# Attention scores from fp16 splits of scaled latents and queries, with two small jobs moved between VectorE and ScalarE

## The reference

```python
q_c = layernorm(x) @ Wq_c.T + bq_c                        # 192 latents
q = (q_c @ Wq_up.T + bq_up).reshape(b, s, 32, 192)
kv = layernorm(x) @ Wkv_c.T + bkv_c                       # 64 key/value latents, 64 rope columns
k_nope, v = split(kv[..., :64] @ Wkv_up.T + bkv_up)       # 128 and 128 per head
k = concatenate([k_nope, kv[..., 64:]])                   # rope columns shared by the heads
scores = einsum('bhqd,bhkd->bhqk', q, k) / sqrt(192)
o = einsum('bhqk,bhkv->bhqv', softmax(scores), v)
x = x + einsum('bhsv,Hv->bsH', o, Wo) + bo
x = x + ffn(layernorm(x))
```

## Time and profile before

| what | value |
|---|---|
| median of 3 runs | 1978.44 us (1977.9 to 1979.36) |
| the profiled execution | 1978.39 us, its span 1976.4 us |
| PE busy | 1937.1 us, 98% |
| DVE busy | 1622.0 us, 82% |
| ACT busy | 1353.8 us, 68% |
| POOL busy | 1102.3 us, 56% |
| mean granted TensorE clock | 0.992 of 2.4 GHz |

### The profile page before, as it was taken

How to read it: one execution, slowest core, us unless ns; L and a number is a source line. 1 busy time by engine, 2 the same in 40 slices (tenths; PEclk the granted TensorE clock), 3 DMA queues, 4 the chain that set the end, 5 groups by cost and what they waited for, 6 DMA issues and landing times. The chain is left out here.

```text
span 1976.4 us, 37173 instructions
## 1 busy us (share of the span) xinstructions
PE 1937.1 (98%) x11014; PEld 1441.7 (73%) x11014; DVE 1622.0 (82%) x2585; ACT 1353.8 (68%) x2488; POOL 1102.3 (56%) x1215
## 2 busy tenths in 40 slices
PE   7999999999999999999999999999999999999798
PEld 6767777777777777777777777777777777777576
DVE  6588888888888888888888888888888888888665
ACT  4367777777777777777777777777777777777443
POOL 3336566565665665655656656656656566565710
PEclk9899999999999999999999999999999999999899
DMA  5521111111111111111111111111111111111211
GB/s 201 194 62 32 43 40 34 43 34 41 44 33 43 40 35 43 36 39 43 34 42 43 32 43 40 35 43 36 40 43 32 43 39 35 43 34 33 75 43 43
DMA packets 74308, 95.19 MB, mean 48 GB/s; under 512 B 25856, under 2 KB 48416, under 8 KB 74272
## 3 DMA queue, kind: packets, MB, share of 16 engines
q1 hardware_dynamic: 70176, 86.33, 17.1%
q0 software_dynamic: 4096, 8.40, 1.2%
HBM read 83.95 MB, written 10.75 MB: 48 GB/s over the span
## 5 line engine op out<-in xcount | busy, mean ns | idle before, releaser
L832 DVE TENSOR_TENSOR PTL<-X,PTH 128x512 f16<-128x512 f32 x1024 | 658.6, 685 | 147.8 <-ACT PTH L783 142.0
L783 ACT ACTIVATE PTH<-X 128x512 f16<-128x512 f32 x1024 | 554.3, 594 | 281.5 <-PE X L692 281.5
L848 DVE TENSOR_REDUCE mx<-S 128x1 f32<-128x1024 f32 x512 | 623.6, 1218 | 3.0 <-PE S L712 3.0
L798 ACT ACTIVATE prob<-S,shift 128x1024 f32<-128x1024 f32 x512 | 574.2, 1121 | 1.7 <-DVE shift L856 1.6
L692 PEld LDWEIGHTS X<-ident,prob 128*128 128x128 f32 x4096 | 469.2, 141 | 120.6 <-issue 53.3
L692 PE MATMUL X<-ident,prob 128*128 128x128 f32 x4096 | 538.1, 274 | 5.3 <-ACT prob L798 5.3
L710 PE MATMUL S<-kvTH,qeH 128*128 128x512 f32 x1024 | 445.5, 435 | 1.6 <-DVE qeL L837 1.6
L712 PE MATMUL S<-kvTH,qeL 128*128 128x512 f32 x1024 | 406.0, 396 | 0.0
L711 PE MATMUL S<-kvTL,qeH 128*128 128x512 f32 x1024 | 401.9, 392 | 0.0
L658 POOL TENSOR_TENSOR onormH<-osum,recip_row 128x512 fp32r<-128x512 f32 x128 | 198.5, 1551 | 288.7 <-ACT osum L806 288.7
L643 POOL TENSOR_TENSOR wvH<-wv,unit_tile 128x128 fp32r<-128x128 f32 x128 | 57.4, 448 | 393.4 <-PE V L763 387.7
(11 more groups left out here) (202 smaller groups left out, 1972.2 us busy)
## 6 DMA issues: line engine op xcount, KB each, us to landing
recip_row<-row_scratch SPq DMA_DIRECT2D x128, 256.0 KB, 4.2
weff<-weff_scratch SPq DMA_DIRECT2D x128, 192.0 KB, 4.0
wv<-in_wv POOLq DMA_DIRECT2D x128, 64.0 KB, 3.7
raw<-in_raw SPq DMA_DIRECT2D x8, 772.0 KB, 5.2
weff_scratch<-w_split SPq DMA_DIRECT2D x8, 768.0 KB, 4.8
x<-in_x SPq DMA_DIRECT2D x4, 1024.0 KB, 6.8
x_all<-in_x SPq DMA_DIRECT2D x3, 1024.0 KB, 6.8
out<-y SPq DMA_DIRECT2D x3, 1024.0 KB, 4.2
```

Source lines behind the costliest of these rows:

```text
L783: nc.scalar.activation(PTH[p][:, part:part + 4, unit * P:(unit + 1) * P], X[:, k % 2, :].rearrange("p (k c) -> p k c", k=4), ACT.Copy).the ...
L798: nc.scalar.activation(prob[u][:], S[:, u % 2, :], ACT.Exp, bias=shift[:, col:col + 1], accum_out=rs[:, col:col + 1]).then_inc(probs_ready, 1)
L832: v.tensor_tensor(PTL[p][at], X[:, k % 2, :].rearrange("p (k c) -> p k c", k=4), PTH[p][at], ALU.subtract).then_inc(low_out, 1)
L848: v.reduce_max(mx[:, col:col + 1], S[:, u % 2, :], AX.X).then_inc(max_ready, 1)
```

## The change

The scores' operands become fp16: `kvTH`, `kvTL`, `qeH` and `qeL`, which were fp32r (fp32 storage). So that fp16 can hold them, the key latents and the queries are scaled by powers of two, and the exponential undoes it by a factor `unscale`.

- `prepare`: all 128 key latents are scaled on ACT where they are read out (`read_projected`), with `scale` and `kbias` made on DVE before. To scale the queries, DVE takes the largest entry of each group's effective weights (two `reduce_max` in `split_absorbed`), and a chain of small steps between DVE and PE (`reach_of_queries`, `scale_of_queries`, three matmuls of one or 128 columns) makes `qscale` and `unscale`.
- `attention`, queries: ACT writes the scaled queries twice from `O`, once as fp32 `qef` and once as fp16 `qeH`, both with a factor and a bias from memory. DVE forms `qeL` from these two, in phase 3 instead of phase 1, and no longer reads `O`. PE waits for `q_high` instead of `q_low` before it writes over `O`.
- `attention`, shift: DVE writes the row's `top` (the same kind of instruction as before). ACT makes `shift` from it by an activation on 128x1, waits for its own result, and runs the exponential with `unscale` as a factor from memory.

```diff
@@ -145,7 +154,9 @@
...
@@ -256,24 +268,29 @@
...
-                pe.wait_ge(wabs_ready, 2)
+                pe.wait_ge(wabs_ready, 1)
                 for k in range(KT):
-                    last = mm(psN[:, UN * KVL:UN * KVL + 1], wabs[:, k, :], ones[:], start=(k == 0), stop=(k == KT - 1))
+                    last = mm(psN[:, B0:B0 + 1], wabs[:, k, 0:P], ones[:], start=(k == 0), stop=(k == KT - 1))
                 last.then_inc(bound_done, 1)
                 pe.wait_ge(wlL_ready, 1)
...
-                pe.wait_ge(diag_ready, 1)
                 for u in range(UN):
-                    last = mm(psN[:, u * KVL:(u + 1) * KVL], kvf[0:KVL, u * P:(u + 1) * P], diag[:], start=True, stop=True)
+                    last = nc.tensor.transpose(psN[:, u * KVL:(u + 1) * KVL], kvf[0:KVL, u * P:(u + 1) * P], ident[0:KVL, 0:KVL])
                 last.then_inc(n_done, 1)
 
             def turn(n, nxt):
                 if nxt is None:
                     project(n, (0,))
+                    pe.wait_ge(wabs_ready, 3)
+                    for c in (1, 2):
+                        for k in range(KT):
+                            last = mm(psT[0][:, c - 1:c], wabs[:, k, c * P:(c + 1) * P], ones[:], start=(k == 0),
+                                      stop=(k == KT - 1))
+                    last.then_inc(qbound_done, 1)
                     absorb(n, 0)
                     project(n, (1,))
...
@@ -304,6 +321,16 @@
...
+                if n == 1:
+                    pe.wait_ge(q_step, REACH)
+                    pe.wait_ge(n_out, NB + 1)
+                    mm(psN[:, B0 + 1:B0 + 2], ones_all[:], reach[:, 0:1], start=True, stop=True).then_inc(reach_done, 1)
+                if n == 2:
+                    pe.wait_ge(q_step, TERM)
+                    pe.wait_ge(proj_out, 3 * NB)
+                    mm(psB[0:1, 0:P], term[:], ident[:], start=True, stop=True).then_inc(term_turned, 1)
+            pe.wait_ge(q_step, TOP)
+            mm(psN[:, B0 + 2:B0 + 3], ones_all[0:1, :], top[0:1, :], start=True, stop=True).then_inc(top_spread, 1)
...
                 nc.scalar.activation(wlH[:], wl[:], ACT.Copy).then_inc(wlH_ready, 1)
-                for half in range(2):
-                    nc.scalar.activation(wabs[:, :, half * KVL:(half + 1) * KVL], wl[:, :, 0:KVL],
-                                         ACT.Abs).then_inc(wabs_ready, 1)
-                nc.scalar.activation(pbabs[:], pb[:, 3:4], ACT.Abs).then_inc(wabs_ready, 1)
+                nc.scalar.activation(wabs[:, :, 0:P], wl[:, :, 0:P], ACT.Abs).then_inc(wabs_ready, 1)
+                nc.scalar.activation(pbabs[:], pb[:], ACT.Abs).then_inc(wabs_ready, 1)
                 read_turned(n, range(UN))
+                nc.scalar.activation(wabs[:, :, P:3 * P], wl[:, :, P:3 * P], ACT.Abs).then_inc(wabs_ready, 1)
...
                 for j in which:
                     out, src, hi = ((kvf, psA, "kvTH"), (qaf, psB, "qaH"), (qbf, psC, "qbH"))[j]
                     act.wait_ge(proj_done, 3 * n + j + 1)
-
-                    nc.scalar.activation(out[:], src[:], ACT.Identity, bias=pb[:, j:j + 1])
-                    nc.scalar.activation(keep[hi][:, tok], src[:], ACT.Identity, bias=pb[:, j:j + 1]).then_inc(proj_out, 1)
+                    if j == 0:
+                        act.wait_ge(k_scaled, 1)
+                    factor, bias = (scale[:, 0:1], kbias[:, 0:1]) if j == 0 else (1.0, pb[:, j:j + 1])
+                    nc.scalar.activation(out[:], src[:], ACT.Identity, bias=bias, scale=factor)
+                    nc.scalar.activation(keep[hi][:, tok], src[:], ACT.Identity, bias=bias, scale=factor).then_inc(proj_out, 1)
...
                 high, low = split[i][:, :, 0, :], split[i][:, :, 1, :]
+                v.reduce_max(wmax[:, ds(g, 1), 0], full[:, :, 0, :], AX.XY, apply_absolute_value=True)
+                v.reduce_max(wmax[0:QB, ds(g, 1), 1], full[0:QB, :, 1, :], AX.XY, apply_absolute_value=True)
                 v.tensor_copy(high, full[:, :, 0, :]).then_inc(half_done, 1)
                 v.tensor_copy(split[i][0:QB, :, 2, :], full[0:QB, :, 1, :]).then_inc(half_done, 1)
...
-            def scales_of_values():
+            def scales_of_latents():
...
-                v.tensor_scalar(diag[:], ident[0:KVL, 0:KVL], scale[0:KVL, 0:1], None, ALU.mult).then_inc(diag_ready, 1)
+                v.tensor_scalar(kbias[:], pb[:, 0:1], scale[:, 0:1], None, ALU.mult).then_inc(k_scaled, 1)
+
+            def reach_of_queries():
+
+                dve.wait_ge(qbound_done, 1)
+                v.scalar_tensor_tensor(out=bound[:, 1:3], in0=psT[0][:, 0:2], scalar=NORM_MAX, in1=pbabs[:, 1:3],
+                                       op0=ALU.mult, op1=ALU.add).then_inc(q_step, 1)
+                dve.wait_ge(split_done, groups + 1)
+                v.reduce_max(wtop[:], wmax[:].rearrange("p g s -> p s g"), AX.X).then_inc(q_step, 1)
+                dve.wait_ge(q_step, 2)
+                v.tensor_tensor(reach[:, 1:2], wtop[:, 1:2], bound[:, 2:3], ALU.mult).then_inc(scale_out, 1)
+                dve.wait_ge(scale_out, 3)
+                v.scalar_tensor_tensor(out=reach[:, 0:1], in0=wtop[:, 0:1], scalar=bound[:, 1:2], in1=reach[:, 1:2],
+                                       op0=ALU.mult, op1=ALU.add).then_inc(q_step, 1)
+
+            def scale_of_queries():
+
+
+                dve.wait_ge(bias_in, 16)
+                v.tensor_scalar(keep["beff"][KVL:P, :], bqr[KVL:P, :], SCALE, None, ALU.mult).then_inc(q_step, 1)
+                dve.wait_ge(q_step, 4)
+                v.reduce_max(btop[:], keep["beff"][:], AX.X, apply_absolute_value=True).then_inc(q_step, 1)
+                dve.wait_ge(q_step, 5)
+                dve.wait_ge(reach_done, 1)
+                v.scalar_tensor_tensor(out=term[:], in0=psN[:, B0 + 1:B0 + 2], scalar=btop[:, 0:1], in1=kinv[:],
+                                       op0=ALU.add, op1=ALU.mult).then_inc(q_step, 1)
+                dve.wait_ge(term_turned, 1)
+                v.reduce_max(top[0:1, :], psB[0:1, 0:P], AX.X).then_inc(q_step, 1)
+                dve.wait_ge(top_spread, 1)
+                v.tensor_scalar(qpower[:], psN[:, B0 + 2:B0 + 3], TINY, None, ALU.max).then_inc(q_step, 1)
+                dve.wait_ge(q_step, 8)
...
+                v.tensor_tensor(keep["qscale"][:], qpower[:], kinv[:], ALU.mult).then_inc(q_step, 1)
+                dve.wait_ge(q_step, 12)
+                v.tensor_scalar(keep["beff"][:], keep["beff"][:], keep["qscale"][:, 0:1], None, ALU.mult)
 
             def head(n):
                 norm(n)
                 low_turned(n, range(UN))
-                scales_of_values()
+                scales_of_latents()
...
+                    reach_of_queries()
...
-            dve.wait_ge(bias_in, 16)
-            v.tensor_scalar(keep["beff"][KVL:P, :], bqr[KVL:P, :], SCALE, None, ALU.mult)
+            scale_of_queries()
...
-        qeH = [sb(f"qeH{i}", [P, BLK], F32R) for i in range(2)]
-        qeL = [sb(f"qeL{i}", [P, BLK], F32R) for i in range(2)]
+        qef = [sb(f"qef{i}", [P, BLK]) for i in range(2)]
+        qeH = [sb(f"qeH{i}", [P, BLK], F16) for i in range(2)]
+        qeL = [sb(f"qeL{i}", [P, BLK], F16) for i in range(2)]
...
@@ -747,7 +820,7 @@
                                start=True, stop=True).then_inc(projected0, 1)
                     if u == 1 and one:
                         if exists(g + 1) and on:
-                            pe.wait_ge(q_low, g + 2)
+                            pe.wait_ge(q_high, g + 2)
                         pe.wait_ge(high_out, event(g, 2))
                         pv_high(0, 4)
                         pe.wait_ge(high_out, event(g, 3))
@@ -785,17 +858,24 @@
 
             def high_q(nxt, h, i):
                 act.wait_ge(q_filled, nxt + 1)
-                nc.scalar.activation(qeH[i][:], O[:], ACT.Identity, bias=keep["beff"][:, ds(h, 1)]).then_inc(q_high, 1)
+                bias, factor = keep["beff"][:, ds(h, 1)], keep["qscale"][:, 0:1]
+                nc.scalar.activation(qef[i][:], O[:], ACT.Identity, bias=bias, scale=factor)
+                nc.scalar.activation(qeH[i][:], O[:], ACT.Identity, bias=bias, scale=factor).then_inc(q_high, 1)
 
             high_q(0, 0, 0)
 
             def body(g, b, h, par):
                 on, one, two = exists(g), exists(g - 1), exists(g - 2)
 
-                def exp(head, u, i):
+                def exp(head, hh, u, i):
                     col = i * UN + u
+                    act.wait_ge(top_ready, 4 * head + u + 1)
+                    lifted = keep["c_lift"][:, ds(hh * UN + u, 1)]
+                    nc.scalar.activation(shift[:, col:col + 1], top[:, col:col + 1], ACT.Identity, bias=lifted,
+                                         scale=-1.0).then_inc(shift_ready, 1)
                     act.wait_ge(shift_ready, 4 * head + u + 1)
                     nc.scalar.activation(prob[u][:], S[:, u % 2, :], ACT.Exp, bias=shift[:, col:col + 1],
+                                         scale=keep["unscale"][:, 0:1],
```

(55 more changed lines are left out.)

28 lines of the change are left out of this document (18 added, 10 removed).

## The result

The changed kernel takes 2106.05 us (median of 4 runs, 2104.69 to 2108.3) where the kernel before took 1978.47 beside it: ratio 1.0646, 95% interval 1.0627 to 1.0664. It is 6.5% slower. Forecast were 2110 us and a range of 2020 to 2165.

A forecast was written before the change was run, and what follows sets the result against it. PE bounds the kernel now; after the change ACT's loop, 3.40 us against PE's 3.24, would set the pace. 1978.4 + 120 (steps) + 12 (setup) = 2110 us, range 2020 to 2165.

The forecast's parts named there:

- What bounds: Attention step: PE is the path; ACT's idle time is mostly the loop through PE, leaving about 0.4 us per phase.
- PE's saving: Attention, PE: faster score matmuls and a shorter first of each six save about 0.47 us per step (bounds 0.29, 0.65).
- The shift: Attention, ACT, each exponential: small activation 0.28, own wait 0.10, factor from memory 0.09; together 0.47 us per phase.
- The queries: Attention, ACT: two activations with two pointers, 1.36 us, make copies of phase 0 to phase 1 take 4.33 us.
- The new step: Attention: phase 0 to 1 takes 4.33 us, the other three 3.40 each; 14.53 against 13.59 us, +120 us in all.
- The Trainium skill's pointer rule: ACT: each operand read through a 128x1 pointer adds about 93 ns to an activation, the second as the first.
- DVE and the rest at nothing: Attention: moved `qeL`, DVE, POOL and transfers cost nothing; late low parts would cost 0.1 to 0.3 us per step.
- The setup: `prepare`: added maxima on DVE cost 8.5 us and the queries' scale chain 3.5, together +12 us (bounds 5 and 20).
- Small additions: Rival, ACT in attention: cheap shift and free second pointers, 0.22 us per phase, total 2010 us; chance 0.20.
- Large additions: Rival, ACT in attention: 0.66 us per phase, step 15.10 us, setup 20 us, total 2191 us; chance 0.08.
- PE stays the path: Rival, attention: PE still sets the pace, step 13.12 us, kernel faster at 1930 us; chance 0.04.
- The clock: Rival, attention: PE's gaps lower its granted clock; in a tenth of the steps 130 us more, 2240 us; chance 0.04.

## Why the prediction was right

**What bounds.** Right. The idle time of ScalarE was the loop's way through PE; with 0.41 us more per phase the loop and not PE sets the pace, and PE waits for the exponential. One sign came only in part: PE was to wait in every phase, and the profile shows it idle only ahead of phase 2. From start to start phase 3 is 3.42 us against 3.24 with the shift back on VectorE, phase 0 is 3.41 against 3.38, so PE does lose 0.18 and 0.03 us there.

**PE's saving.** Taken 0.47 us per step, measured 0.38 (types alone). The score matmul's spacing gives about what was reckoned, 0.014 each for 0.012. The first of each six was to give 0.012 + 0.045 and gives 0.02: it holds its place for 908.78 - 908.56 = 0.22 us instead of 0.32, but starts 0.87 instead of 0.79 behind the first transpose. In phase 1 of the changed kernel nothing of it is to be seen (2.27 us for transposes and scores, as before), mostly because the transposes' weights come late there.

**The shift.** Taken 0.47 per phase: 0.28 + 0.10 + 0.09. Measured 0.33 for activation and wait (299 ns, then 0.04 us), and 0.08 in the span of exponential and row sum (1.29 to 1.30 us for 1.21 to 1.22). The exponential itself is 83 ns longer, by the groups' means 1204 against 1121; the row sum starts 1.10 instead of 1.00 us behind the exponential and is 23 ns shorter. Sum 0.41, a loop of 3.34 instead of 3.40 us. The term that was mis-sized is the wait for its own result, taken 0.10, measured 0.04.

**The queries.** Taken 4.33 us from the copies of phase 0 to those of phase 1. By rows the spacings of the two activations are 0.68 and 0.66 us, and a step of 14.50 less 3.34, 3.41 and 3.42 leaves 4.33. Right.

**The new step.** Taken 4.33 + 3 x 3.40 = 14.53, measured 14.49. The agreement is closer than its parts: the loop is 0.06 shorter than reckoned, but where it comes near PE's own time the late weight load adds 0.07 to it (copies 3.41 and 3.42 apart in phases 3 and 0). That loss was not in the prediction; that it makes up for most of the 0.06 is luck. What PE loses per step, taken over 1.4 us, is 14.49 - 13.21 = 1.28 against the types alone.

**The Trainium skill's pointer rule** ("ScalarE: Activation LUTs", section "What ACT_TABLE_LOAD costs", about 93 ns for each such operand) holds for the second as for the first: 687 to 777 ns in the activation of the queries, 1115 to 1203 ns in the exponential.

**DVE and the rest at nothing.** Right: `qeL` waits 3.8 us in all, the low parts of phase 3 come behind it without delaying a transpose. It was closer than it looks: in the kernel whose VectorE also casts, a slow `top` beside GpSimd does cost 0.85 us in 11 steps.

**The setup.** Taken 12 us, measured 10 to the first activation of the queries and 11.1 to the first exponential (113.9 - 102.8); the division into 8.5 and 3.5 is not confirmed. Behind the last exponential the changed kernel takes 139.3 us instead of 137.3, which nothing in the prediction stands for.

**The rivals.** *Small additions* fell by the pointer's price. *Large additions* fell too: the small activation starts 958.43 - 958.32 = 0.11 us before the copies end, as the exponential did (0.12), so this overlap was not lost, and the wait is 0.04, not 0.15. *PE stays the path* did not happen here; nearest to it is the kernel with both repairs: without shift and second activation on ScalarE the step is 13.32 us. *The clock* stayed at 1.00 in the step's window, with gaps of up to 0.74 us of PE in each step.

**Where the gain went.** fp16 gives 1980.0 - 1930.3 = 50 us. The changed kernel pays 1.28 x 128 = 164 us for ScalarE's additions and some 10 us of setup: 1980 - 50 + 174 = 2104, measured 2106. (The 1.28 is itself a difference of measured steps, so this sum says where the time lies and does not test the parts.) Of the ScalarE part, the shift's move and the second activation each give back 0.57 to 0.58 us per step when undone, and 1.17 together; 0.11 remain between both repairs and the types alone, most likely the factors from memory of the exponential and of the queries' activation (argued, not tried by themselves in that kernel).

**The version that beats both** is the kernel before with fp16 for these four tensors: 0.9747 [0.9731, 0.9763]. It has no scaling, so it relies on latents and queries that fit fp16's range as they are. The kernel with both repairs keeps the scaling and is still 1.2% faster than before, but its shift leaves out the rounding with the row's bias, so it is not quite the same computation.

## What to carry to other kernels

An engine's idle share is no room if its idle time is one leg of a loop through another engine. Add up the loop (here copies, exponential, the way back: 2.92 us) and compare it with the bounding engine's time for the same round (3.36); only the difference is free. Work that makes a faster form possible for the bounding engine should not go to the engine next to it in that loop beyond that difference, and an instruction on 128x1 is not small: it costs 0.33 us with its own wait, a fourth of an exponential over 1024 columns.

## What had not been expected of the hardware

- ScalarE's wait for its own result costs 0.04 us (958.61 to 958.65) beyond the lost overlap, like VectorE's shortest (0.03) and not like its longest (0.15).
- The transposes' weight load did not pass ahead of their wait: where the wait ended within some 0.1 us of PE's coming free, the transposes started 0.13 us behind the exponential (959.94 to 960.07) instead of 0.05 (956.60 to 956.65), and a phase is up to 0.14 us longer than PE's own 3.28. Why it is 0.13 there and not 0.05 no run shows.
- The row sum's read takes 190 ns behind the waiting exponential and 213 ns behind one that follows the copies directly.
- Beside instructions of GpSimd, `top` on VectorE, an instruction on 128x1, took up to 1.59 us instead of 0.22, and the cast of the queries 0.39 to 1.51 us with a median of 1.30. Not every one that runs beside GpSimd is longer, and what decides it is open.
